# The down product of a mixture-of-experts layer three items behind gate and up, with pad rows stored by SyncE

## What is computed

```python
mod = silu(c) @ wmod                                # shifts, scales and gates sa, ca, ga, sb, cb, gb
h = layernorm(x) * (1 + ca) + sa
x = x + ga * linear_attention(h)                    # 16 heads of 32, relu(q), relu(k), then a projection
h = layernorm(x) * (1 + cb) + sb
x = x + gb * moe(h)

def moe(h):                                         # 8 experts, hidden size 512, the best 2 of each token
    logits = (rmsnorm(h) * router_scale) @ router   # [tokens, 8]
    probs, choices = softmax(logits), top2(logits)
    # each chosen expert, on its own tokens only:
    act = gelu(h @ gate[e]) * (h @ up[e])
    out = (act @ linear[e]) * per_expert_scale[e]
    # summed over the two experts with probs renormalised over the chosen two
```

## Time and profile before

| | |
|---|---|
| median of 3 runs | 2235.86 us |
| profiled execution, its own time | 2233.56 us |
| its span | 2231.7 us |
| granted TensorE clock, mean | 0.97 of full |
| TensorE (PE) busy | 2084.5 us, 93% |
| VectorE (DVE) busy | 1336.0 us, 60% |
| ScalarE (ACT) busy | 809.4 us, 36% |
| GpSimd (POOL) busy | 809.7 us, 36% |
| phase 3, first matmul to last | 1033 to 2224 us |

### The profile page before, as it was taken

The page is one execution under the profiler, slowest core; times in us unless marked ns, Lnnn a source line. Parts: engine busy times, 40 slices in busy tenths (PEclk is TensorE's granted clock), DMA queues, the critical chain, the costliest instruction groups (busy, mean ns, idle before and its releaser), DMA issues.

```text
span 2231.7 us, 42442 instructions
## 1 busy us (share of the span) xinstructions
PE 2084.5 (93%) x9408; PEld 1628.5 (73%) x9409; DVE 1336.0 (60%) x3182; ACT 809.4 (36%) x1493; POOL 809.7 (36%) x626
## 2 busy tenths in 40 slices
PE   7999999999989999984899998998999989999997
PEld 5688887888846666653788887887778778778885
DVE  6556564556268878863565565665556556556664
ACT  3244443444345666651233232332223223223332
POOL 4466756576415676643111111111111111111111
PEclk9999999999989999986999999999999999999999
DMA  7576564655535676675855557557675775765554
GB/s 247 186 243 207 194 205 147 201 185 203 179 139 205 221 265 242 237 273 172 230 128 129 124 127 224 127 128 221 169 183 129 226 224 127 194 161 129 131 117 78
DMA packets 293177, 404.89 MB, mean 181 GB/s; under 512 B 50510, under 2 KB 188750, under 8 KB 285262
## 3 DMA queue, kind: packets, MB, share of 16 engines
q1 hardware_dynamic: 165104, 257.57, 36.1%
q0 software_dynamic: 30640, 74.29, 15.8%
q10 hardware_dynamic: 97200, 70.82, 10.0%
HBM read 210.57 MB, written 191.98 MB: 180 GB/s over the span
## 4 chain that ended last, share of the span: by engine, by line
PE 43%; DMA 7%; DVE 2%; issue 1%; ACTq 1%; ACT 0%; DVEq 0%; POOL 0%; SPq 0%; POOLq 0%
PE bank L1722 43%; DMA act_rows<-hact 3%; DMA arow<-act_rows 3%; DMA out_rows<-orow,cur_tok 1%; ACTq L1035 1%; DVE hact L1611 0%; DVE gbr L1647 0%; DVE x_t_lo L1605 0%; DVE act_t_lo L1622 0%; DVE orow L1650 0%; DVEq L1629 0%; ACT gact L1024 0%; DMA expert_rows<-rows,dest 0%; DMA meta<-expert_rows 0%; POOL expert_rows L741 0%
## 5 line engine op out<-in xcount | busy, mean ns | idle before, releaser
L1722 PE MATMUL bank<-wbuf,x_t_hi 128*128 x2160 | 678.7, 396 | 42.1 <-DVE x_t_lo L1605 41.6
L771 POOL DMA_INDIRECT out_rows<-orow,cur_tok x135 | 209.0, 1548 | 986.1 <-DVE orow L1650 904.1
L1722 PEld LDWEIGHTS bank<-wbuf,x_t_hi 128*128 128x128 f32 x2160 | 408.7, 190 | 136.4 <-issue 46.2
L1722 PE MATMUL bank<-wbuf,x_t_lo 128*128 x1080 | 424.8, 393 | 0.0
L1722 PE MATMUL bank<-wbuf,act_t_hi 128*128 x1080 | 347.4, 404 | 36.6 <-DVE act_t_lo L1622 36.6
L1611 DVE TENSOR_TENSOR hact<-bank,gact 128x512 f32<-128x512 f32 x135 | 93.3, 691 | 326.2 <-PE bank L1722 301.5
L1722 PEld LDWEIGHTS bank<-wbuf,act_t_hi 128*128 128x128 f32 x1080 | 208.3, 194 | 87.2 <-issue 41.2
L1722 PEld LDWEIGHTS bank<-wbuf,x_t_lo 128*128 128x128 f32 x1080 | 204.3, 189 | 45.9
L1722 PE MATMUL bank<-wbuf,act_t_lo 128*128 x540 | 216.3, 401 | 0.0
L1024 ACT ACTIVATE gact<-bank 128x512 f32<-128x512 f32 x135 | 80.7, 598 | 323.7 <-PE bank L1722 250.5
L1019 ACT ACTIVATE x_t_hi<-bank 128x512 fp32r<-128x512 f32 x135 | 80.9, 599 | 261.0 <-PE bank L1722 252.0
(11 more groups left out here) (219 smaller groups left out, 3887.2 us busy)
## 6 DMA issues: line engine op xcount, KB each, us to landing
wbuf<-expert_split SPq DMA_DIRECT2D x24, 1536.0 KB, 9.0
xrow<-expert_rows SPq DMA_DIRECT2D x540, 64.0 KB, 3.2
act_rows<-hact ACTq DMA_DIRECT2D x135, 256.0 KB, 2.2
arow<-act_rows ACTq DMA_DIRECT2D x540, 64.0 KB
expert_split<-split_hi SPq DMA_DIRECT2D x32, 768.0 KB, 3.5
expert_split<-split_lo SPq DMA_DIRECT2D x32, 768.0 KB, 5.9
xg<-in_x SPq DMA_DIRECT2D x16, 1024.0 KB, 5.6
q_rows<-qf SPq DMA_DIRECT2D x16, 1024.0 KB, 6.7
```

Source lines behind the costliest of these rows:

```text
L771: pool.indirect_dma_start(out=out, out_offset=bass.IndirectOffsetOnAxis(cur_tok[at][:, 0:1], 0), in_=orow[at % 2][:, :], in_offset=None, c ...
L1722: last = mm(dst, stationary(a, f), moving(b, f), start=(first and k == 0), stop=(k == parts * n - 1))
```

## The change

It has four parts.

1. **The down product lags by three items.** TensorE's order becomes `gate(i)`, `up(i)`, `down(i - 3)`. On VectorE `turn_act`, `act_lo` and `out_rows` take one item more of lag each. On ScalarE `act_back(i - 1)` moves from ahead of `gelu(i)` to behind `x_hi(i + 1)`, with `act_hi` and `gb_rows` one item later.
2. **Doubled places.** `hact` and `arow` are double, `act_rows` has four places, the small tiles `cur_w`, `in_b0`, `in_b1` four and `cur_tok` eight; the waits that guarded the old number of places ask for less.
3. **The router in the last group of phase 2.** On TensorE `logits(14)` moves ahead of the third projection and `rank(14)` into the middle of the fourth; on ScalarE the copy of the logits moves ahead of a square; on VectorE the weights and places of group 14 move from the end of the group to ahead of the fourth `residual`.
4. **Pad rows by SyncE.** All eight pads become direct stores that SyncE issues when `pad_to` is ready; SyncE waits for them behind the barrier, before it loads the rows of any item.

```diff
@@ constants, buffers @@
+LAG = 3
...
-    ad = nc.dram_tensor("act_rows", (2 * P, H), F32, kind="Internal").ap()
+    ad = nc.dram_tensor("act_rows", (RING * P, H), F32, kind="Internal").ap()
...
-    hact = sb(ph3, "hact", [P, H], F32)
-    cur_w, in_b0, in_b1 = ([sb(ph3, f"{n}{i}", [P, 1], F32) for i in range(2)] for n in ("cur_w", "in_b0_", "in_b1_"))
-    cur_tok = [sb(ph3, f"cur_tok{i}", [P, 1], U32) for i in range(RING)]
+    cur_w, in_b0, in_b1 = ([sb(ph3, f"{n}{i}", [P, 1], F32) for i in range(RING)] for n in ("cur_w", "in_b0_", "in_b1_"))
+    cur_tok = [sb(ph3, f"cur_tok{i}", [P, 1], U32) for i in range(DEPTH)]
-    arow = sb(ph3, "arow", [P, H], F32)
+    arow = [sb(ph3, f"arow{i}", [P, H], F32) for i in range(2)]
+    hact = [sb(ph3, f"hact{i}", [P, H], F32) for i in range(2)]
...
@@ SyncE @@
         for n in DOWNS:
             load_weights(0, 0, n)
+        sp.wait_ge(s_padi, 3)
+        for e in range(E):
+            r = sp.value_load(pad_to[0:1, e:e + 1], min_val=0, max_val=E * CAP)
+            sp.dma_start(xs[bass.ds(r, P), :], padrow[:, :]).then_inc(s_pad, 16)
         phase2_over(sp)
+        sp.wait_ge(s_pad, 16 * E)
...
-                share(k, i - 1 if SHARES[k] == DOWNS else i)
+                share(k, i - LAG + 1 if SHARES[k] == DOWNS else i)
...
-        load_rows(0, 0)
-        sp.wait_ge(s_pad, 16 * (E - 1))
-        for i in range(1, AHEAD):
+        for i in range(AHEAD):
             load_rows(i, i)
@@ GpSimd @@
-        pool.wait_ge(s_padi, 3)
-        def pad(e):
-            return pool.indirect_dma_start(out=xs, out_offset=bass.IndirectOffsetOnAxis(pad_to[:, e:e + 1], 0),
-                                           in_=padrow[:, :], in_offset=None)
-        pad(0).then_inc(s_pad0, 16)
         scatter(NG - 1, 1)
-        for e in range(1, E):
-            pad(e).then_inc(s_pad, 16)
@@ ScalarE @@
+            if before_it and not more:
+                logits_out(g - 1)
             square(g, 0, par)
-            if before_it:
+            if before_it and more:
                 logits_out(g - 1)
...
         def store_act(i, at):
-            wait_apart(act, s_ar, 16 * NBLK * (i - 1))
+            wait_apart(act, s_ar, 16 * NBLK * (i - RING + 1))
             wait_apart(act, s_h, i + 1)
...
         def act_back(i, at):
-            wait_apart(act, s_ht, i)
+            wait_apart(act, s_ht, i - 1)
             wait_apart(act, s_hst, 16 * (i + 1))
...
         def item(i, at):
-            lagging = not isinstance(i, int) or i > 1
+            lagging = not isinstance(i, int) or i >= LAG
             if lagging:
-                act_hi(i - 2)
-            act_back(i - 1, at - 1)
+                act_hi(i - LAG)
             gelu(i)
             if more:
                 x_hi(i + 1, at + 1)
+            act_back(i - 1, at - 1)
             store_act(i, at)
             if lagging:
-                gb_rows(i - 2, at)
+                gb_rows(i - LAG, at - LAG)
@@ VectorE @@
             if router:
                 choice(g - 1)
+            if last:
+                all_weights(g - 1, 1 - par)
+                all_places(g - 1, 1 - par)
             residual(g, 3, par)
...
-            if router and last:
-                all_weights(g - 1, 1 - par)
-                all_places(g - 1, 1 - par)
...
-            at_least(dve, s_hst, 16 * i)
-            tt(hact[:, :], U_B[:, :], gact[:, :], ALU.mult).then_inc(s_h, 1)
+            at_least(dve, s_hst, 16 * (i - 1))
+            tt(hact[at % 2][:, :], U_B[:, :], gact[:, :], ALU.mult).then_inc(s_h, 1)
...
         def item(i, at):
             cur_of(i - 1, (at - 1) % DEPTH)
             if lagging:
-                act_lo(i - 2)
+                act_lo(i - LAG)
             if more:
                 turn_x(i + 1, (at + 1) % DEPTH)
-            glu(i)
+            glu(i, at)
             if more:
                 x_lo(i + 1, at + 1)
-            turn_act(i - 1)
+            if lagging or i == LAG - 1:
+                turn_act(i - LAG + 1, (at - LAG + 1) % DEPTH)
             if lagging:
-                out_rows(i - 2, (at - 2) % DEPTH)
+                out_rows(i - LAG, (at - LAG) % DEPTH)
@@ TensorE @@
+            if not has(g, 1):
+                logits(g - 1)
+                project(g, par, 2)
+                turn_logits(g - 1)
+                project(g, par, 3, between=lambda: rank(g - 1))
+                return
...
-            if not isinstance(i, int) or i > 1:
-                down(i - 2, expert_of(i - 2))
+            if not isinstance(i, int) or i >= LAG:
+                down(i - LAG, expert_of(i - LAG))
```

More of the change, by code:

```diff
@@ L774, in _ @@
         item(0, 0)
-        run_items(pool, item)
+        run_items(pool, item, DEPTH)
         pool.wait_ge(s_add, 16 * ITEMS)
@@ L1062, in item @@
                 x_hi(i + 1, at + 1)
+            act_back(i - 1, at - 1)
             store_act(i, at)
             if lagging:
-                gb_rows(i - 2, at)
+                gb_rows(i - LAG, at - LAG)
         run_items(act, item)
-        act_hi(ITEMS - 2)
-        act_back(ITEMS - 1, ITEMS - 1)
-        gb_rows(ITEMS - 2, ITEMS - 2)
-        act_hi(ITEMS - 1)
-        gb_rows(ITEMS - 1, ITEMS - 1)
+        for i in range(ITEMS - LAG, ITEMS):
+            act_hi(i)
+            if i == ITEMS - LAG:
+                act_back(ITEMS - 1, ITEMS - 1)
+            gb_rows(i, i)
     @block.vector
@@ L1655, in _ @@
         turn_x(1, 1)
-        glu(0)
+        glu(0, 0)
         x_lo(1, 1)
@@ L1715, in _, with product @@
         turn(0, 3)
-        def product(dst, parts, n, stationary, moving, first=True):
+        def product(dst, parts, n, stationary, moving, first=True, between=None):
             k = 0
@@ L1723, in product @@
                     k += 1
+                    if between and k == parts * n // 2:
+                        between()
             return last
@@ L1875, in rank, with project @@
             last.then_inc(s_rank, 1)
-        def project(g, par, t):
+        def project(g, par, t, between=None):
             b = batch_of(g)
@@ L1886, in project @@
             product(dst, 3, FC, lambda a, f: on[par][a][:, f, t * P:(t + 1) * P],
-                    lambda k, f: kvp[k][:, b, f, :], first=False).then_inc(s_y, 1)
+                    lambda k, f: kvp[k][:, b, f, :], first=False, between=between).then_inc(s_y, 1)
         def turn_h2(g, par, t):
@@ L1935, in group2 @@
                 logits(g - 1)
-            if has(g, 1):
-                spread(g + 1, 2)
-                spread(g + 1, 3)
+            spread(g + 1, 2)
+            spread(g + 1, 3)
             if not before_it:
@@ L1997, in item @@
             up(i, e)
-            if not isinstance(i, int) or i > 1:
-                down(i - 2, expert_of(i - 2))
+            if not isinstance(i, int) or i >= LAG:
+                down(i - LAG, expert_of(i - LAG))
         run_items(pe, item)
-        for i in range(ITEMS - 2, ITEMS):
+        for i in range(ITEMS - LAG, ITEMS):
             down(i, expert_of(i))
```

47 lines of the change are left out of this document (24 added, 23 removed).

## The result

The change runs in **2219.68 us** (median of 4 runs, 2217.47 to 2228.31) against 2237.03 us for the kernel before on the same chip (median of 4). The ratio is 0.9938 with a 95% interval of 0.9914 to 0.9962: faster by 14 to 17 us, where 44 were forecast. The prediction, 2192 us and at most 2215, was wrong in size and right in sign.

The account below looks back on a forecast made before the run. Bound: engines waiting for DMAs late beside phase 3's weight loads, 58.0 us. Stalls -41, ends of phase 3 +3, hand-over -6 from 2233.56 gave 2189.6, or 2192 us against the median; own range 2173 to 2211, wider range 2172 to 2215.

Parts of the forecast that it names:

- What bounds the kernel: Phase 3: weight loads make DMAs late, VectorE stands still for them and TensorE then waits; cost 58.0 us.
- The stall term: Phase 3 beside weight loads: one item more of lag hides most late stores and loads; -41 us, ends -58 and -28.
- the 58: Six phase 3 stretches with weight loads: 445.34 us against 387.3 at 8.24 us an item, the pool to gain from.
- The quiet pace: Phase 3 items away from weight loads: must stay at 8.24 us each; if longer, rival C is right.
- rival C: ScalarE's `gb` behind the four issues delays the path to `act_t_lo`: slower, 2238 to 2271 us, taken 2245; chance 0.05.
- Doubled places of `hact`: Phase 3: `hact` no longer waits for the previous item's store; part of the 58, not counted apart.
- Both ends of phase 3: Start -0.9 us; end gains a down product and waits for `act_t`; taken +3 us, ends +2 and +5.
- The hand-over: Phase 2 to phase 3: earlier last scatter and pads by SyncE bring -6 us, ends -7 and -3.
- A: Phase 3: DMA engines become the bound, or the output's add falls behind; 2213 to 2220 us, taken 2216; chance 0.20.
- The share of 0.84: Highest DMA busy share seen, in the longest weight-load stretch; as a limit it gives the stall gain's -28 us end.
- D: TensorE's late waits come from something other than the round trip, so lag only moves them; 2231 us; chance 0.04.

Follow-up runs that it names:

- thin_weights: tiles_behind with the weight loads of experts 1 to 7 cut to 16 columns, so those weights are wrong; 2177.4 us, 0.9727 of the kernel before.
- gb_first: tiles_behind with `gb` on ScalarE ahead of the four issues of `arow` and of the store; 2200.55 us, 0.9801 of the kernel before.
- tiles_behind: The change with its ten added small tiles moved behind `hact`, so `wbuf` lies at byte 95168 again; 2219.8 us, 0.9892 of the kernel before.
- after: The change itself, all four parts on the kernel before, as profiled; median 2219.68 us, profiled execution 2228.31 us, ratio 0.9938.
- old_order: The change with the four loads of `arow` ahead of gelu again on ScalarE, lag still three; 0.9946 of the kernel before.
- places_only: The kernel before with `hact` and `arow` doubled and four places of `act_rows`, lag still two; 0.9975 of the kernel before.
- lag_only: Parts 1 and 2 of the change (lag of three, doubled places) alone on the kernel before; 0.9960 of the kernel before.
- store_first: tiles_behind with ScalarE's order `x_hi`, store, `gb`, then the issues of `arow`, and semaphores for each parity of items; 2195.11 us, 0.9794 of the kernel before.

## Why the prediction was right or wrong

**What bounds the kernel: right.** The long items are the weights' traffic (thin_weights: 1.3 us left of 43.2), and what is late is a DMA for which an engine stands still in its order.

**The stall term: wrong, and the largest error.** The forecast kept 17 us of the 58; the change kept 36.2 (31.8 in its second profile) of what, counted by items of over 8.55 us, was 61.3. The step that failed is that a store of up to 6.6 us and a load of up to 10.1 us cost nothing and a longer one only its excess, taken with "The chain holds four stores over 6.6 us". The limit itself is near: an item of 8.24 us has room for a store of 6.0 us and 2.2 us of issues. But I had priced a late store as lateness of that item alone, against a time at which the store leaves that stays put. In the new order the next store stands behind the loads that wait for this one, so that each late store starts the next one late: 1598.32, 1609.60, 1620.83 us. And I had counted the stores on before's chain, four, and not all those issued beside weights. The other half of the same step is `gb`. I put it behind the four issues at 1.94 us, with 0.8 us to spare on the path to `act_t_lo`, and counted only issue time; ScalarE stands ahead of those issues until the store has landed. gb_first, which only moves `gb`, takes 19 us off tiles_behind.

The Trainium skill (DMA: Bandwidth & Descriptors, Anatomy of one DMA) says that the wait for a semaphore happens on the issuing sequencer, ahead of the DMA. The trace agrees: the store of 1598.32 us lands at 1607.37, and the loads that wait for it go out at 1607.46, with the next store and `gb` behind them, though `hact` was ready since 1605.0. Everything written behind a waiting issue is behind a transfer.

**The quiet pace: wrong.** The sum went by 8.24 us an item on both sides. In after it was 8.36, 12.4 us more in the rest of the items (0.9 to 13.3). Nothing in rival C's mechanism makes it: old_order has the same pace. The prediction said that a longer quiet pace would prove C right; that was a false test. It came with the doubled places of four small tiles, the part of the change that I had costed at nothing, through the address of the tile behind them. That it cost so little in time may be because the stalls shrank beside it; the profiles give 5 us for that, no more than two profiles of one kernel differ by.

**Doubled places of `hact`: right.** They had no gain of their own in the forecast, and places_only has none in its long items (64.2 us against 61.3).

**Both ends of phase 3: about right.** The forecast was +3 with -0.9 at the start and some +3.4 at the end. The end cost 4.4 us; the waits were 2.5, 1.9 and 1.9 us where 2.6, 1.9 and 1.9 stood in the forecast.

**The hand-over: in the range, the middle too good.** -6 was forecast, -7 to -3 the ends, and -4.0 came at the first matmul. The places of group 14 came 7.3 us earlier. The last places, "which nothing here moves", came 1.8 us later. And the last scatter took longer: two of its issues lasted 1.75 and 1.92 us, where the others take about 1.0. SyncE's eight pads, which took 9.58 us to issue where I had 8, are not the reason. lag_only has no pads on SyncE and shows the same two, and there as here each stands beside one of VectorE's 128x945 operations on the item tables:

```profile
1018.52 1.15 DVE L1581 TENSOR_TENSOR h2t<-item_no,cnt 128x945 f32<-128x945 f32 x1
1018.79 1.72 POOL L742 DMA_INDIRECT expert_rows<-rows,dest  x1 [0.30 <-issue]
...
1020.76 1.13 DVE L1583 TENSOR_TENSOR h2t<-h2t,cnt 128x945 f32<-128x945 f32 x1
1020.82 1.90 POOL L742 DMA_INDIRECT expert_rows<-rows,dest  x1 [0.30 <-issue]
```

In the kernel before, that work fell beside the scatter of group 14, where one issue took 1.51 us, and not beside the last. That the scatter lands last was right.

**The rivals.** A gave 2216 us for the reason that stretches stay costly; its time, 2213 to 2220, is what came, and its sign, late output adds, shows in after ([3.41 <-DMA out_rows<-orow,cur_tok] above). But its reason is not the one: the DMA engines are not the bound in general, since store_first moves the same bytes with 15 us of long items and passes a whole set of weights at a DMA share of 0.88 without one. The share of 0.84, which the slow end of the forecast's range took as a limit, is none. Only around 1722 to 1795 us, where TensorE waits for the weights themselves, may the transfers be the limit. C's mechanism was there, and its place: `gb` behind the issues. It bites only where a store is late and not in every item, so that it costs about 20 us and not 46 or more. D's time should have been 2233 us by its own terms (2233.56 + 3 - 6 + 2.3), not 2231; nothing hangs on it.

**The sum.** Long items -25.1, other items +12.4, first `hact` -3.2 (less the 6.1 us), the end +4.4, and the 6.1 us of earlier phases: -5.4, against -5.5 between the two spans.

## What to carry to other kernels

Before moving a DMA issue that waits, list what stands behind it on its queue: if the next transfer of the same kind is there, they run one at a time, and the period is a transfer plus the issues, however much lag the consumer was given. A lag helps in full only if every leg can be under way twice; here the lag alone gave 9 us, and a better order of `gb`, store and loads on top of it about 20 more. And compare the addresses of the large operands before and after an edit of buffers: small tiles ahead of them can change the pace of every matmul.

## What the runs showed of the hardware

- The same 36 matmuls of 128x512 float32r, each with its own weight load, take 8.24 us (229 ns each) with the moving operand at byte 95168 or 97216 of a partition, and 8.36 us (232 ns) at 95488 or 95232, at a granted clock of 1.00. The Trainium skill (TensorE: Matmul & The Clock Gate, Wait — 56ns, not 53.3ns?) gives 215.7 ns from start to start for back-to-back matmuls of 512 columns at 2.4 GHz, and names no type of number; the fastest stretches here, of float32r, have 229.
- A third pace, 8.40 us (233 ns), sets in or ends at a stall and then holds for as long as there is none, in one run and not in another of the same kernel.
- A store of 256 KB takes 9 us beside a weight load (9.05 and 8.98 in after), where the median of all in the kernel before is 2.2.
- An indirect DMA issue of GpSimd takes 1.7 to 1.9 us beside a VectorE operation of 128x945, where others take 1.0 (1.75 and 1.92 in after, 1.72 and 1.90 in lag_only).
